# Conditional linear layer with a residual: twelve instead of sixteen slices of the conditioned weights in fp32, their bf16 parts laid out by burst, and loads in another order

## The chip, the core and the metric

One NeuronCore of one Trainium2 chip runs the kernel. The metric is the device time of one execution in microseconds. SyncE and ScalarE issue the transfers, each from a queue of its own; all of them share the core's 16 DMA engines.

## The reference

```python
def reference(x, cond_8, L0_cond_weight, L0_cond_mask, L0_cond_bias):
    # x (128, 128, 512), cond_8 (128, 8), weight (8, 512, 512), mask (512, 512), bias (512,), all fp32
    masked_w = weight * mask[None, :, :]
    w_bot = jnp.einsum('bg,got->bot', cond_8, masked_w)
    return x + jnp.einsum('bnt,bot->bno', x, w_bot) + bias
```

Each of the 128 batches gets its own 512 x 512 matrix, a mix of eight, and multiplies its 128 rows of x with it. The kernel adds the residual by adding the identity to the matrix.

## The kernel before

**Units, steps, groups.** A unit is 32 batches by 128 output columns; there are 16 (`UNITS`), units 0 to 3 for the first 32 batches, and so on. A unit has eight steps, so `n` runs over 128 steps. In step `n`, `group(n)` multiplies four batches of x with their matrices: 16 fp32 matmuls of 128 x 128 x 128, each of which the profile shows as two records of MATMUL. x lies in eight buffers of 1 MB (`xs`), one for four batches, and stays for four units. The first set is x loads 0 to 7, the next is 8 to 15 (`load_x`, at the steps in `X_AT`), and group 32 is the first to use x load 8, group 39 the first to use x load 15.

**Bursts.** The matrices of the next unit are made beside the groups, in bursts: burst `b` makes 16 output columns for 32 batches, eight bursts a unit (`bursts_before(n)` names those that TensorE runs ahead of group `n`). A burst has four chunks of one PSUM bank (`ps1`, six banks). Two kinds exist:
- the first `FB` = 16 bursts, units 0 and 1, in fp32 (`first_burst`, line 529). Eight run before step 0. VectorE evicts them, times the mask (line 465), and GpSimd adds the identity (`add_one`, line 374);
- the other 112 in bf16 (`burst`, line 549), with the masked weights split in three bf16 parts (w1, w2, w3) and the conditioning values too. ScalarE evicts them (line 406). The contraction has 98 rows: 6 products of parts (`Y_PART`) of 16 rows each, and two rows of the identity (`eye`). So a slot of `ring` holds, by partition, w1, w2, w1, w2, w1, w3 and the identity.

**Parts.** A tile is 128 x 512 masked weights; there are 32 of them, in 8 halves of 4, a half for 4 bursts. For tile `t`, SyncE loads it (`load_raw`, two at a time), VectorE multiplies the mask (line 449), ScalarE casts to w1 (line 397), GpSimd subtracts (line 365) and makes w3 (line 367), ScalarE makes w2 (line 401), and SyncE stores all three to `scratch` in memory (`store_parts`, line 269). `TILES_AT` sets the step in which the engines work at a tile. There are five buffers of parts: the cast of tile `t` waits until tile `t - 5` is stored (`stored`, line 218).

**Loads of a burst.** `load_burst` waits for the four tiles of its half to be stored (while they are first needed) and for its slot in the ring of six, then issues the identity rows (line 286), w1 and w2 in one load of 256 KB to partitions 0 to 31 (line 289), w3, 128 KB to 80 to 95 (line 290), and, for the first 24 bursts (`thrice`), w1 again, 128 KB to 64 to 79 (line 293). VectorE copies partitions 0 to 31 to 32 to 63 (line 455) and, for the other 88 bursts, w1 to 64 to 79 in a second copy (line 457).

**What sets the order.** Each engine runs its list in order, written out by the loops over `n`. SyncE's list is the one in which a wait holds up all transfers behind it, except those that ScalarE issues (stores of the result, line 411).

## Time and profile before

| | |
|---|---|
| three runs, us | 640.91, 646.6, 647.01; median 646.6 |
| the profiled execution | 643.54 us, span 641.1 us |
| granted TensorE clock, mean | 0.997 |
| VectorE, ScalarE, GpSimd busy | 411.7, 297.0, 110.2 us |
| bytes moved | 144.44 MB, 225 GB/s over the span |

The page's 40 slices (16 us each) show TensorE busy from the third slice to the end, GpSimd at work until slice 13, and the DMA engines at their fullest up to slice 15:

```profile
PE   6999999999999899999999999999999999999997
POOL 4594586353431000000000000000000000000000
PEclk9999999999999989999999999999999999999999
DMA  8959979999989796455599984555599985652112
```

To read it: a digit is the busy share of a slice in tenths, PEclk the granted clock, DMA the mean busy share of 16 engines. A share of 1.0 in the windows below says that no DMA engine had a gap. "x32" behind a matmul counts records, two to an fp32 matmul.

### The profile page before, as it was taken

The page shows a single profiled execution, that of the slowest core. Times are in us where ns is not written, and L with a number is a line of the kernel's source. Part 1 is how long each engine was busy: PE and PEld are TensorE (multiplying, and loading weights), DVE is VectorE, ACT ScalarE, POOL GpSimd, SP SyncE. Part 2 cuts the span into 40 slices and gives each one's busy share as a digit, 9 for nine tenths or more (in the row PEclk, how much of TensorE's full clock was granted, in tenths as well). Part 3 has the DMA queues.
Part 4 walks back from the last instruction along what each step waited for, and adds up shares of the span by engine and source line. Part 5 has one row for each costly group of instructions (what it writes and reads, how often), then busy time and mean ns, then how long its engine had stood idle before and what let it go on. Part 6 is the DMA issues. An engine that isn't in the chain of part 4 may idle for free.

```text
span 641.1 us, 18487 instructions
## 1 busy us (share of the span) xinstructions
PE 629.0 (98%) x7808; PEld 594.3 (93%) x7808; DVE 411.7 (64%) x425; ACT 297.0 (46%) x513; POOL 110.2 (17%) x95
## 2 busy tenths in 40 slices
PE   6999999999999899999999999999999999999997
PEld 2466779999999899999999999999999999999997
DVE  4986777556655567766776667666676676667421
ACT  0131226666666354445545545455445544554500
POOL 4594586353431000000000000000000000000000
PEclk9999999999999989999999999999999999999999
DMA  8959979999989796455599984555599985652112
GB/s 319 398 176 358 323 219 295 304 330 308 294 278 329 249 292 198 136 162 153 150 271 299 316 236 139 150 155 160 137 238 316 320 248 141 169 150 97 51 67 82
DMA packets 63649, 144.44 MB, mean 225 GB/s; under 512 B 8078, under 2 KB 33776, under 8 KB 53360
## 3 DMA queue, kind: packets, MB, share of 16 engines
q1 hardware_dynamic: 44624, 109.34, 58.0%
q10 hardware_dynamic: 18944, 33.93, 15.6%
q8 instruction: 62, 1.02, 0.7%
q14 instruction: 19, 0.16, 0.1%
HBM read 97.10 MB, written 46.14 MB: 223 GB/s over the span
## 4 chain that ended last, share of the span: by engine, by line
PE 93%; DMA 3%; DVE 2%; issue 1%; ACT 1%; SPq 0%; ACTq 0%; DVEq 0%
PE ps L568 70%; PE ps L549 15%; PE ps L529 7%; DMA w_parts<-parts 2%; DVE wbot L465 1%; DVE raw L449 1%; ACT wbot L406 1%; DMA first_sb<-in_first 1%; DMA ring<-w_parts 1%; DVE ring L457 0%; DVE yblk L484 0%; DVE staged L478 0%; SPq L301 0%; SPq L286 0%; DVE ring L455 0%
## 5 line engine op out<-in xcount | busy, mean ns | idle before, releaser
L568 PE MATMUL ps<-wbot,xs 128*128 128x128 f32 x4096 | 478.2, 277 | 0.8 <-DVE wbot L465 0.4
L568 PEld LDWEIGHTS ps<-wbot,xs 128*128 128x128 f32 x4096 | 466.0, 193 | 5.5 <-issue 4.7
L406 ACT ACTIVATE wbot<-ps 128x512 f32<-128x512 f32 x448 | 259.5, 610 | 224.2 <-PE ps L568 115.8
L478 DVE TENSOR_TENSOR staged<-ps,bias_sb 128x512 f32<-128x512 f32 x128 | 88.5, 691 | 197.8 <-PE ps L568 197.6
L455 DVE COPY ring<-ring 32x4096 bf16<-32x4096 bf16 x112 | 137.2, 1225 | 7.3 <-DMA ring<-w_parts 3.9
L549 PE MATMUL ps<-ydiag,ring 98*128 98x64 bf16 x3584 | 117.2, 193 | 2.8 <-DVE ring L457 2.5
L549 PEld LDWEIGHTS ps<-ydiag,ring 98*128 98x128 bf16 x3584 | 114.8, 98 | 4.3 <-issue 2.6
L457 DVE COPY ring<-ring 16x4096 bf16<-16x4096 bf16 x88 | 107.2, 1218 | 2.7
L365 POOL TENSOR_TENSOR raw<-raw,parts 128x512 f32<-128x512 f32 x32 | 45.7, 1428 | 68.9 <-ACT parts L397 68.8
L465 DVE TENSOR_TENSOR wbot<-ps,ring 128x512 f32<-128x512 f32 x64 | 43.1, 687 | 14.1 <-PE ps L529 10.4
L397 ACT ACTIVATE parts<-raw 128x512 bf16<-128x512 f32 x32 | 19.7, 623 | 50.4 <-DVE raw L449 33.3
L367 POOL TENSOR_TENSOR parts<-raw 128x512 bf16<-128x512 f32 x32 | 39.1, 1221 | 2.5
L449 DVE TENSOR_TENSOR raw<-raw,mask_sb 128x512 f32<-128x512 f32 x32 | 36.6, 1155 | 0.5
L401 ACT ACTIVATE parts<-raw 128x512 bf16<-128x512 bf16 x32 | 20.0, 625 | 35.3 <-POOL raw L365 33.0
L529 PE MATMUL ps<-yblk,xs 128*128 128x512 f32 x64 | 30.2, 636 | 5.2 <-DVE yblk L484 5.2
L529 PEld LDWEIGHTS ps<-yblk,xs 128*128 128x128 f32 x64 | 13.0, 205 | 21.6 <-issue 15.6
L529 PE MATMUL ps<-yblk,ring 128*128 128x512 f32 x64 | 28.6, 592 | 0.0
L529 PEld LDWEIGHTS ps<-yblk,ring 128*128 128x128 f32 x64 | 11.6, 190 | 12.0 <-issue 11.7
L374 POOL TENSOR_TENSOR wbot<-wbot,first_sb 128x512 f32<-128x512 f32 x16 | 20.8, 1300 | 7.4 <-DVE wbot L465 7.2
L484 DVE TENSOR_TENSOR yblk<-first_sb 128x512 f32<-128x512 f32 x1 | 0.7, 691 | 4.5 <-DMA first_sb<-in_first 4.5
L397 ACT ACT_TABLE_LOAD x1 | 1.3, 1283 | 2.7 <-issue 2.7
L355 POOL TENSOR_SCALAR staged<-staged,pick_sb 98x128 bf16<-98x128 bf16 x3 | 1.8, 602 | 0.3
(10 smaller groups left out, 4.0 us busy)
## 6 DMA issues: line engine op xcount, KB each, us to landing
xs<-in_x SPq DMA_DIRECT2D x32, 1024.0 KB, 12.0
out<-staged ACTq DMA_DIRECT2D x128, 256.0 KB, 4.0
ring<-w_parts SPq DMA_DIRECT2D x112, 256.0 KB, 5.7
ring<-w_parts SPq DMA_DIRECT2D x136, 128.0 KB, 6.6
w_parts<-parts SPq DMA_DIRECT2D x32, 384.0 KB, 9.3
raw<-in_w SPq DMA_DIRECT2D x16, 512.0 KB, 9.3
ring<-in_w SPq DMA_DIRECT2D x4, 512.0 KB, 14.9
ring<-in_eye SPq DMA_DIRECT2D x112, 16.0 KB
```

The costliest lines, as they stand in the source:

```text
L365: eng.tensor_tensor(at, at, w1, ALU.subtract).then_inc(s_rest, 1)
L367: eng.tensor_tensor(parts[:, t % PARTN, 2, :, :], at, high_half(t), ALU.subtract).then_inc(s_p3, 1)
L397: eng.activation(parts[:, t % PARTN, 0, :, :], raw[:, t % RAWN, :, :], ACT.Copy).then_inc(s_p1, 1)
L406: eng.activation(chunk_place(b, k), chunk_sums(b, k), ACT.Copy).then_inc(s_ev_a, 1)
L449: eng.tensor_tensor(at, at, mask_sb[:, h % 2, :].unsqueeze(1).to_broadcast([P, TG, TW]), ALU.mult).then_inc(s_mul, 1)
L455: eng.tensor_copy(ring[2 * ROWS:4 * ROWS, i, :], ring[0:2 * ROWS, i, :]).then_inc(s_dup, 1)
L457: eng.tensor_copy(ring[4 * ROWS:5 * ROWS, i, :], ring[0:ROWS, i, :]).then_inc(s_dup, 1)
L465: eng.tensor_tensor(at, ps1[(b * KT + k) % S1B][:, :].rearrange("p (b o) -> p b o", o=CO), mask_t_sb[:, k, o:o + CO].unsqueeze(1).to_broad ...
L478: eng.tensor_tensor(staged[:, n % OUTB, :].rearrange("p (b o) -> p b o", b=GB), ps2[n % S2B][:, :].rearrange("p (b o) -> p b o", b=GB), bi ...
L529: ins = eng.matmul(ps1[(b * KT + k) % S1B][:, :], raw01_sb[u][:, c, k * P:(k + 1) * P], yblk[:, :], start=True, stop=True)
L549: ins = eng.matmul(ps1[at % S1B][:, g * W * OJ:(g + 1) * W * OJ], ring[0:KALL, i, k * CW + g * P:k * CW + (g + 1) * P], ydiag[:, first:fir ...
L568: ins = eng.matmul(ps2[n % S2B][:, b * SL:(b + 1) * SL], xs[:, load % GROUPS * GB + b, k, :], at, start=(k == 0), stop=(k == KT - 1))
```

## The change

Only bursts 0 to 11 are made in fp32 (`FB` = 12, a unit and a half). Bursts 12 to 15, the second half of slice 1, are made from bf16 parts; the order of the halves is turned so that theirs is prepared first. Bursts 12 and 13 stand ahead of group 6, 14 and 15 ahead of group 7, and step 5 has none. `scratch` is laid out by burst: for each of the four bursts of a half its w2, w1 and w3, 16 rows of 8 KB each, one behind the other. So one load takes w2 and w1 (to partitions 0 to 31), another w1 and w3 (to 64 to 95), each 256 KB from memory without a gap, and every burst has both; the three-load form and VectorE's second copy are gone. A tile now holds 512 columns of one kind in place of two times 256, so a store writes runs of 1 KB and not of 512 bytes, and a mask is 256 KB and not 128 (its multiplication reads it without repeating). `TILES_AT` takes tiles 6 to 15 a little earlier and tiles 17 to 31 at closer steps; a tile is stored one step behind its making (two from step 8 on); before, it was two throughout. SyncE issues x loads 2 to 5 ahead of the first stores, x load 6 behind them, x load 7 in step 0, and within a step stores ahead of x loads. The second set's x loads stand at steps 26, 27, 29, 30, 31, 33, 34, 35 in place of 25, 26, 27, 28, 30, 31, 32, 34. `yblk` and the fp32 weights of unit 1 move within the ring.

The core of the diff:

```diff
-FB = FU * CS
+FB = CS + CS // 2
...
 HALVES = 2 * SLICES
+CH = CS // 2
 TG = 2
 TILES = HALVES * NG // TG
 PER_HALF = NG // TG
-TW = 256
-HCOLS = P // OJ * TW
+TW = 512
...
+PART1, PART2, PART3 = 1, 0, 2
...
 EARLY = 4
-TILES_AT = {0: (4, 5), 1: (6,), 2: (7, 8), 3: (9,), 4: (10, 11), 5: (12,), 6: (13, 14), 7: (15,),
-            **{8 + (t - 16) * 7 // 5: (t,) for t in range(16, TILES)}}
+TILES_AT = {0: (4, 5), 1: (6, 7), 2: (8, 9), 3: (10, 11), 4: (12,), 5: (13,), 6: (14,), 7: (15,),
+            **{8 + (t - 16) * 5 // 4: (t,) for t in range(16, TILES)}}
+STORE_AT = {}
+for _n, _tiles in TILES_AT.items():
+    STORE_AT[_n + (1 if _n < GROUPS else 2)] = STORE_AT.get(_n + (1 if _n < GROUPS else 2), ()) + _tiles
...
     if n < GROUPS:
-        return ((), (8,), (9,), (10,), (11,), (12,), (13,), (14, 15))[n]
+        return ((), (8,), (9,), (10,), (11,), (), (12, 13), (14, 15))[n]
...
-X_AT = {_g: LAST_USE[_g - _g % GROUPS - GROUPS] + 1 + _g % GROUPS * 9 // 7 for _g in range(GROUPS, XLOADS)}
+X_AT = {_g: LAST_USE[_g - _g % GROUPS - GROUPS] + 2 + (_g % GROUPS * 4 + 1) // 3 for _g in range(GROUPS, XLOADS)}
...
-    return 2 * ((s - FU) % SLICES) + c // KT
...
+    return (2 * s + c // CH - FB // CH) % HALVES
+def fresh(b):
+    return b < FB + SLICES * CS
...
-    return (half_of(u % SLICES, c) + 1) * PER_HALF if u < FU + SLICES else 0
+    return (half_of(u % SLICES, c) + 1) * PER_HALF if fresh(b) else 0
...
-    return (4, 5, 0, 2, 3, 1)[(b - FB) % RING]
-def thrice(b):
-    return b < FB + 3 * CS
+    return (4, 5, 0, 3, 2, 1)[(b - FB) % RING]
...
 def free_before(b):
     r = b - FB
-    if r < 3:
+    if r < 4:
         return 0
-    if r == RING - 1:
-        return GROUPS
     last = FB - 1 if r < RING else b - RING
-    return next(n for n in range(STEPS) if LAST_BURST[n + 1] >= last)
+    return next(n for n in range(STEPS) if LAST_BURST[n + 1] >= last) + (r == RING - 1)
...
-        yblk = sb("yblk", [P, BANK], fp32)
...
-                    ring[:, 2:4, :].rearrange("p i c -> p (i c)").bitcast(fp32).rearrange("p (c t) -> p c t", c=CS)]
+                    ring[:, 2, :].bitcast(fp32).rearrange("p (c t) -> p c t", c=FB - CS)]
+        yblk = ring[:, 1, BW // 2:BW // 2 + 2 * BANK].bitcast(fp32)
...
-                at = scratch[h, 0, i, 0, :]
-                to = bass.AP(tensor=at.tensor, offset=at.offset, ap=[[TW, P], [ROWS // TG * HCOLS, 3 * TG], [1, TW]])
-                eng.dma_start(to, parts[:, t % PARTN, :, :, :].rearrange("p j g c -> p (j g) c"))\
-                   .then_inc(s_store[t % PARTN], 16)
+                at = scratch[h, 0, 0, i * TG * OJ, :]
+                to = bass.AP(tensor=at.tensor, offset=at.offset, ap=[[TW, P // CH], [3 * ROWS * BW, CH], [ROWS * BW, 3], [1, TW]])
+                eng.dma_start(to, parts[:, t % PARTN, :, :]).then_inc(s_store[t % PARTN], 16)
             def load_burst(b):
                 u, c = divmod(b, CS)
                 s, i = u % SLICES, slot_of(b)
                 h = half_of(s, c)
-                if u < FU + SLICES:
+                if fresh(b):
                     for t in range(h * PER_HALF, (h + 1) * PER_HALF):
                         stored(eng, t)
                 if b >= FB + RING:
                     eng.wait_ge(s_s1, (b - RING + 1) * KT)
-                elif b >= FB + 5:
+                elif b == FB + 5:
                     eng.wait_ge(s_ev_v, FB * KT)
-                elif b >= FB + 3:
+                elif b == FB + 4:
                     eng.wait_ge(s_s1, FB * KT)
                 ones = (KT - 1 - s) * CW // 2
                 eng.dma_start(ring[KROWS:KALL, i, :].bitcast(fp32), eye[c, :, ones:ones + BW // 2]).then_inc(s_eye[i], 16)
-                w1_w2 = scratch[h, 0:2, :, :, c % KT * BW:(c % KT + 1) * BW].rearrange("j g o c -> (j g o) c")
-                w3 = scratch[h, 2, :, :, c % KT * BW:(c % KT + 1) * BW].rearrange("g o c -> (g o) c")
-                eng.dma_start(ring[0:2 * ROWS, i, :], w1_w2).then_inc(s_w12[i], 16)
-                eng.dma_start(ring[5 * ROWS:KROWS, i, :], w3).then_inc(s_w3[i], 16)
-                if thrice(b):
-                    w1 = scratch[h, 0, :, :, c % KT * BW:(c % KT + 1) * BW].rearrange("g o c -> (g o) c")
-                    eng.dma_start(ring[4 * ROWS:5 * ROWS, i, :], w1).then_inc(s_w1[i], 16)
+                w21 = scratch[h, c % CH, 0:2, :, :].rearrange("j r c -> (j r) c")
+                w13 = scratch[h, c % CH, 1:3, :, :].rearrange("j r c -> (j r) c")
+                eng.dma_start(ring[0:2 * ROWS, i, :], w21).then_inc(s_w21[i], 16)
+                eng.dma_start(ring[4 * ROWS:KROWS, i, :], w13).then_inc(s_w13[i], 16)
...
-            load_x(2)
-            load_first(1, 4, 2)
-            load_x(3)
+            for g in range(2, 6):
+                load_x(g)
             for t in range(EARLY):
                 store_parts(t)
+            load_x(6)
             loaded = FB
             kept = 0
             for n in range(STEPS):
-                kept = max((kept, EARLY if n >= 2 else 0, *(t + 1 for t in TILES_AT.get(n - 3, ()))))
-                if n + X_AHEAD < GROUPS:
-                    load_x(n + X_AHEAD)
-                if n == 0:
-                    load_first(1, 6, 2)
+                kept = max((kept, EARLY if n >= 1 else 0, *(t + 1 for t in STORE_AT.get(n - 1, ()))))
                 for t in (8, *TILES_AT[RAW_AHEAD]) if n == 0 else TILES_AT.get(n + RAW_AHEAD, ()):
                     if t >= RAWN and t % 2 == 0:
                         load_raw(t)
+                if n == 0:
+                    load_x(7)
                 while loaded < BURSTS and free_before(loaded) <= n and tiles_of(loaded) <= kept:
                     load_burst(loaded)
                     loaded += 1
+                for t in STORE_AT.get(n, ()):
+                    store_parts(t)
                 for g in range(GROUPS, XLOADS):
                     if X_AT[g] == n:
                         load_x(g)
-                for t in TILES_AT.get(n - 2, ()):
-                    store_parts(t)
...
-                if not thrice(b):
-                    eng.tensor_copy(ring[4 * ROWS:5 * ROWS, i, :], ring[0:ROWS, i, :]).then_inc(s_dup, 1)
...
-                if n == GROUPS - 2:
-                    duplicate(FB)
-                    made += 1
-                while n >= GROUPS and made < BURSTS and made <= n + GROUPS + AHEAD:
+                while n >= GROUPS // 2 and made < BURSTS and made <= n + GROUPS + (AHEAD if n > GROUPS // 2 else 0):
```

SyncE's list from the first stores of tiles on, before (`w_parts` is the scratch in memory; eye, w1 and w2, w3, w1 again are the four loads of a burst; the burst here is 16, then follow 17 and 18 in the same form):

```order
L269 DMA w_parts<-parts 128x6x256 [waits s_p3,s_p2] x4
...
L301 DMA xs<-in_x 128x2048 [waits s_s1]
L246 DMA mask_sb<-in_mask 128x256 [waits s_mul]
L256 DMA raw<-in_w 128x1024 [waits s_p3,s_p2]
L286 DMA ring<-in_eye 2x2048 [waits s_store2,s_store3,s_store1,s_store0]
L289 DMA ring<-w_parts 32x4096
L290 DMA ring<-w_parts 16x4096
L293 DMA ring<-w_parts 16x4096
...
L269 DMA w_parts<-parts 128x6x256 [waits s_p3,s_p2] x2
L301 DMA xs<-in_x 128x2048 [waits s_s1]
```

and now (the burst is 12, then 13, 14 and 15 in the same form; line 266 stores tiles, 294 loads x, 242 a mask, 252 tiles, 282 to 286 a burst):

```order
L266 DMA w_parts<-parts 32x12x512 [waits s_p3,s_p2] x4
...
L294 DMA xs<-in_x 128x2048 [waits s_s1]
L242 DMA mask_sb<-in_mask 128x512 [waits s_mul]
L252 DMA raw<-in_w 128x1024 [waits s_p3,s_p2]
L282 DMA ring<-in_eye 2x2048 [waits s_store2,s_store3,s_store1,s_store0]
L285 DMA ring<-w_parts 32x4096
L286 DMA ring<-w_parts 32x4096
...
L266 DMA w_parts<-parts 32x12x512 [waits s_p3,s_p2] x4
L252 DMA raw<-in_w 128x1024 [waits s_p3,s_p2]
```

Behind the first four stores, four bursts of two loads stand ahead of the next stores (tiles 4 to 7, four in a row), where three bursts of three loads stood ahead of two.

ScalarE's list ahead of its first eviction, before (line 401 makes w2, 397 casts w1 and waits for a stored tile, 411 stores a result, 406 evicts; the steps are 6 to 8):

```order
L401 ACTIVATE parts<-raw 128x512 [waits s_rest]
L397 ACTIVATE parts<-raw 128x512 [waits s_store3,s_mul]
L397 ACTIVATE parts<-raw 128x512 [waits s_store4,s_mul]
L411 DMA out<-staged 128x512 [waits s_o]
L401 ACTIVATE parts<-raw 128x512 [waits s_rest] x2
L397 ACTIVATE parts<-raw 128x512 [waits s_store0,s_mul]
L406 ACTIVATE wbot<-ps_4 128x8x32x2 [waits s_s2,s_s1]
L406 ACTIVATE wbot<-ps_5 128x8x32x2 [waits s_s2,s_s1]
L411 DMA out<-staged 128x512 [waits s_o]
```

and now (line 392 makes w2, 388 casts w1, 402 stores, 397 evicts; the steps are 4 to 6):

```order
L392 ACTIVATE parts<-raw 128x512 [waits s_rest] x2
L388 ACTIVATE parts<-raw 128x512 [waits s_store2,s_mul]
L402 DMA out<-staged 128x512 [waits s_o]
L392 ACTIVATE parts<-raw 128x512 [waits s_rest]
L388 ACTIVATE parts<-raw 128x512 [waits s_store3,s_mul]
L397 ACTIVATE wbot<-ps_0 128x8x32x2 [waits s_s2,s_s1]
L397 ACTIVATE wbot<-ps_1 128x8x32x2 [waits s_s2,s_s1]
L402 DMA out<-staged 128x512 [waits s_o]
```

The first eviction by ScalarE (burst 16 before, burst 12 now) has moved up past the work at tiles 14 and 15: it stands behind the cast of tile 13 and ahead of that of tile 14, where it stood behind the cast of tile 15.

## Rows read from the trace of the kernel before

**Rows 1.** The page, part 1: busy us, share of the span, instructions.
```profile
PE 629.0 (98%) x7808; PEld 594.3 (93%) x7808; DVE 411.7 (64%) x425; ACT 297.0 (46%) x513; POOL 110.2 (17%) x95
```

**Rows 2.** The page, part 5: second copies on VectorE; count, busy, mean ns, idle before.
```profile
L457 DVE COPY ring<-ring 16x4096 bf16<-16x4096 bf16 x88 | 107.2, 1218 | 2.7
```

**Rows 3.** The chain in order of time: start us, us, what was waited for or worked.
```profile
68.46 3.44 PE ps L529 x8
...
82.47 6.87 PE ps L529 x16
...
92.91 0.94 PE ps L549 x32
...
204.31 13.15 DMA w_parts<-parts
...
217.91 3.47 DMA ring<-w_parts
...
225.22 8.86 PE ps L568 x64
...
240.53 3.65 PE ps L568 x32
```

**Rows 4.** Timeline of TensorE: start us, us, work, count, idle before and releaser.
```profile
224.13 1.09 PE L549 MATMUL ps<-ydiag,ring 98*128 98x64 bf16 x32 [2.46 <-DVE ring L457]
```

**Rows 5.** Windows: us; busy of each engine; clock, DMA share, GB/s.
```profile
10.00:30.00 20.00, 20.00 (x47) 8.75 (x47) 16.89 (x25) 1.89 (x3) 12.34 (x14) 1.00 1.02 417
...
60.00:70.00 10.00, 10.00 (x58) 7.15 (x57) 5.99 (x9) 0.00 (x0) 0.00 (x0) 1.00 1.06 257
...
80.00:90.00 10.00, 10.00 (x47) 6.17 (x46) 7.29 (x8) 2.76 (x6) 9.76 (x9) 1.00 0.72 245
...
100.00:200.00 100.00, 99.70 (x1421) 98.95 (x1420) 59.03 (x59) 67.35 (x119) 45.22 (x32) 1.00 1.00 304
...
200.00:220.00 20.00, 20.00 (x251) 19.98 (x250) 12.16 (x12) 9.57 (x17) 0.00 (x0) 1.00 0.85 286
...
260.00:320.00 60.00, 60.00 (x864) 59.89 (x864) 41.42 (x40) 30.64 (x53) 0.00 (x0) 1.00 0.52 148
```

**Rows 6.** Timeline of SyncE: start us, us, DMA issued.
```profile
54.42 0.42 SPq L293 DMA_DIRECT2D ring<-w_parts  x1
...
57.79 0.42 SPq L293 DMA_DIRECT2D ring<-w_parts  x1
...
58.31 0.97 SPq L269 DMA_DIRECT2D w_parts<-parts  x2
...
224.07 0.42 SPq L301 DMA_DIRECT2D xs<-in_x  x1
```

**Rows 7.** Their landings, one line each: L293 twice, L269 (first), L301.
```profile
DMA to landing us min/median/max: 9.9/9.9/9.9
...
DMA to landing us min/median/max: 11.6/11.6/11.6
...
DMA to landing us min/median/max: 12.1/12.1/12.1
...
DMA to landing us min/median/max: 15.5/15.5/15.5
```

**Rows 8.** The page, part 6: x loads, KB each, median us to landing.
```profile
xs<-in_x SPq DMA_DIRECT2D x32, 1024.0 KB, 12.0
```

**Rows 9.** Timeline of ScalarE at the cast of tile 9.
```profile
70.53 0.63 ACT L397 ACTIVATE parts<-raw 128x512 bf16<-128x512 f32 x1 [13.53 <-DMA w_parts<-parts]
```

**Rows 10.** Timeline of GpSimd: the two subtractions of tile 9; one identity added.
```profile
71.24 1.16 POOL L365 TENSOR_TENSOR raw<-raw,parts 128x512 f32<-128x512 f32 x1 [12.67 <-ACT parts L397]
...
72.47 1.04 POOL L367 TENSOR_TENSOR parts<-raw 128x512 bf16<-128x512 f32 x1
...
90.77 1.16 POOL L374 TENSOR_TENSOR wbot<-wbot,first_sb 128x512 f32<-128x512 f32 x1
```

**Rows 11.** Waits of SyncE: us in total, times, longest.
```profile
SPq L218 <- DMA w_parts<-parts: 18.0, 2, 12.4
```

60 lines of the change are left out of this document (26 added, 34 removed).

## The prediction

> **What bounds the kernel now.** I read the page first: TensorE is busy for 629.0 of the span of 641.1 us [rows 1]. So only two things can move the end: less work on TensorE, or other waits of it. The second view is the chain in order of time [rows 3]. It shows what a step costs: an fp32 burst on TensorE 3.44 us (the two of step 7 together 6.87), a bf16 burst 0.94, a group of sixteen fp32 matmuls 3.65. It also shows the one place where TensorE is not the chain: at 204.31 a store of tile 31 is issued, lands 13.15 us later, and only then may the load of burst 44 be issued (3.47 to land); its copy and burst 44 itself follow. TensorE waits 2.46 us for that [rows 4], and the two groups behind it take 8.86 us where two at 3.65 would take 7.3: 1.6 us of lower clock after the wait. So 4.1 us of the span are lost there.
>
> Third, who was late in that place? The windows [rows 5] say: the transfer queues. From 60 to 70 and from 100 to 200 us their share is 1.0 or above; from 260 us on, with no tiles to load or store and no x loads, it is 0.52. Up to 240 us the kernel stands close to two limits, TensorE's and the queues', and after that at TensorE's alone.
>
> **What goes: four fp32 bursts.** Bursts 12 to 15 become bf16: 4 x (3.44 - 0.94) = 10.0 us of TensorE time. With the 4.1 us of waiting gone too, the span would be 641.1 - 4.1 - 10.0 = 627.0. The 88 second copies on VectorE go as well, 107.2 us of it [rows 2]; nobody waited for VectorE but once, at 224, and there for a copy that was itself late by its load. I cost them at nothing; what hides them is TensorE's groups.
>
> **What is added to the queues.** Each bf16 burst now takes two loads of 256 KB, onto 32 partitions each. The nearest rows are the bursts of before that took the same bytes, to the same partitions, in three loads: the last piece of burst 16 is issued at 54.42 and lands 9.9 later, that of burst 18 at 57.79 and 11.6 later [rows 6, 7]. That is 64.3 and 69.4: two bursts in 5.1 us of a full queue, 2.56 each. An x load, 1 MB to 128 partitions, costs 2.5 at the 417 GB/s of the window from 10 to 30 us [rows 5]; in the window from 60 to 70, which is mostly bursts, the same full queue moved 257 GB/s. So bytes of bursts are dear. What the change adds up to x load 15, the last of the second set of eight, needed at group 39:
> - bursts 12 to 15 loaded: 4 x 2.56 = +10.2
> - bursts 40 to 48 load a third piece again, a quarter of 2.56: 9 x 0.64 = +5.8
> - x loads 4 and 5 are ahead of the first store, where the queue has room: -5.0; 512 KB of fp32 weights gone: -1.3
> - six masks of twice the size, 128 KB more each: +1.9
> - 28 stores of the same bytes in half as many pieces. No row shows a store in pieces of 1 KB. Its gain lies between nothing and half of the 0.9 us that 384 KB take at 417 GB/s; I take 0.1 each, since the queue's full windows already move other loads with small pieces among them: -2.8 (ends 0 and -13)
>
> Sum +8.8. Before, x load 15 was issued at 224.07 and landed 15.5 later, at 239.6 [rows 6, 7]; group 39 started at 240.53 [rows 3]. The queues had idle time that a later TensorE would let them use: 2.8 us in 80 to 90 and 3.0 in 200 to 220 [rows 5]. So x load 15 lands at 239.6 + 8.8 - 5.8 = 242.6. Group 39 without waits would start at 240.5 - 4.1 - 10.0 = 226.4. TensorE is thus late by some 16 us there, in several waits, not one: **the gain of 10 us is handed to a queue that cannot go faster.** Behind group 39 the queue has room again: the two later sets of x loads meet no tiles, and 12.0 us of median landing [rows 8] stand against at least four steps of 3.65 to 5.5 us between issue and use.
>
> **The first of these waits, at step 6.** The store of tile 4 is now issued behind four bursts. Before, it was issued at 58.31 and landed 12.1 later, at 70.4 [rows 6, 7], and ScalarE stood 13.53 us for it, in front of its cast of tile 9 [rows 9]. In the changed order the queue ahead of it holds 1.5 MB of x and fp32 weights less (-3.8), a mask's 128 KB more twice (+0.6) and one burst more (+2.6): it lands near 69.8. Behind that cast ScalarE has, before it may evict burst 12: casts of tiles 9 to 13, and these wait for GpSimd, which takes 1.16 + 1.04 for each tile [rows 10] and two additions of the identity of about 1.15 between. From the landing: 0.6 + 2.3 + 1.15 + 2 x 2.3 + 1.15 + 1.2 + 2 x 0.6 = 12.2. Eviction starts at 82.0. TensorE gets to burst 12 at 72.0 (68.46, where the fp32 burst 12 started before, and one group ahead of it) and has six banks, so it stands from 73.4, in the middle of burst 13, until the first eviction ends at 82.6: 9.2 us. Before, VectorE evicted these bursts and no cast stood in front of them. This wait is part of the 16 us and not to be added, since the queue works on meanwhile.
>
> **The sum.** 627.0 + 16.2 + 2 x 1.6 for the clock, lowered after the two longest waits as at 225, = 646.4 of span. The profiled execution took 643.5 at a span of 641.1, so 2.4 lie around it: 648.8. The median of the runs shown is 646.6, so against that the change is +0.3%. About 1% is what a measurement of this kernel can tell from no change: below 640.1 I call faster, above 653.1 slower.
>
> **A rule to weigh.** The row says 2.56 us for 512 KB onto 32 partitions twice, half the rate of x loads. The Trainium skill, "SBUF — State Buffer", section "Door 1: The DMA port swizzle", says that 32 partitions reach 8 of 16 ports, and gives 189 GB/s; by that a burst would cost 2.8 us, an estimate, and the new order in memory would not help. The trace's 2.56 is near it. By the same page 16 partitions reach half as many ports again, so a load of half the bytes would take as long as the full one; the landings of the three pieces do not settle that.
>
> **Rivals.**
> - *Reads from memory were the brake (faster).* Before, a burst's rows lay 32 KB apart; now they lie together. For it: the low rate occurs only with these loads (but so does the narrow destination). Against it: the weights' rows of the fp32 part lie apart too and moved at full rate within the window of 10 to 30 us. If it holds, a burst costs 1.3 us at 417 GB/s, 37 bursts save 46 us, and the queues bind nowhere. The wait at step 6 stays, smaller: the store lands at 69.8 - 4 x 1.26 = 64.8, the first eviction ends at 77.6, 4.2 us late. 627.0 + 4.2 + 1.6 + 2.4 = 635.2.
> - *The third piece is free.* If a load onto 16 partitions already cost what one onto 32 costs, the 5.8 fall away: 643.0. This is the port rule above carried through (same page and section).
> - *SyncE stands for the landing of stores (slower).* Each half's first burst waits until the half's last tile is stored, and SyncE issues nothing meanwhile; at 204 to 218 this let the queue run dry once, 3.5 us from the new load to its landing. In the changed order the store is issued one step ahead of that burst, as before, but the queue is fuller, and x loads 10 to 15 stand behind the last such wait instead of 14 and 15. If three more halves run the queue dry: 3 x 3.5 = 10.5, less the 2 or so that the sum already grants: 657. It decides from the point at which a store lands more than a step after its issue, some 4.6 us; the one at 58.31 took 12.1.
> - *The change doesn't take the fp32 work off the path* is excluded: TensorE's order shows it.
>
> **How the numbers follow.** Forecast (queues full, price of a burst as before) 0.36, its own range 643 to 653; free third piece 0.10; memory reads 0.33; SyncE's standing 0.21. Faster by over 1%: the 0.33 and a little of bursts near 2 us, 0.34. Within 1%: 0.45. Slower: 0.21. Range 634 to 657: from the faster rival to the slower one. The term that decides is the price of a burst: at 1.3 the queue has 30 us to spare, at 2.56 it lacks 16, and it turns near 2.1.
>
> **What will show each step.**
> - TensorE busy about 10 us less for lines of stage 1: 0.94 per burst for 12 to 15.
> - Landings of the two pieces of bursts 12 to 15: 2.5 us from burst to burst means the forecast, 1.3 the faster rival.
> - ScalarE's cast of tile 9 near 70 us (65 in the faster rival), and TensorE's wait inside burst 13 until 82.6 (77.6).
> - Waits of TensorE for x loads at groups 34 to 39, and for the copy of burst 40, with a lowered clock behind them. If TensorE has no wait past 100 us, the queue's account is wrong.
> - After group 39 both profiles should show equal steps: eight groups and eight bursts in 8 x (3.65 + 0.94) = 36.7 us.
> - SyncE's waits for landings of stores: 18.0 us in two waits before [rows 11]; far more would be the slower rival.

## The result, and the profile after

The changed kernel takes 667.6 us (median of 4 runs, 662.8 to 668.4) against 646.2 for the kernel before on the same chip (640.9 to 647.0): a ratio of 1.033, 95% interval 1.026 to 1.041. The prediction was 648.8, or +0.3%, its range 634 to 657; it gave its largest chance (0.45) to a time within 1% of before. The change is 3.3% slower. Here and below, medians are over all executions, and ratios are of the means without the few executions in which the chip was in a slower state.

| | before | after |
|---|---|---|
| span of the profiled execution, us | 641.1 | 660.9 |
| mean granted TensorE clock | 0.997 | 0.985 |
| TensorE busy | 629.0 | 625.5 |
| group 39 starts at | 240.4 | 250.7 |
| from there to the end of the span | 400.7 | 410.3 |

TensorE's busy time fell by the 10.0 us of fp32 work that went, and grew again by the lowered clock (below). The last two lines divide the loss: of the 19.8 us of span, 10.3 are there when group 39 starts, and 9.5 come behind it, where the prediction saw equal steps.

The waits of TensorE in the changed kernel: us in total, times, longest.

```profile
PE ps L551 <- DMA xs<-in_x: 14.1, 6, 4.6
PE ps L532 <- ACT wbot L397: 11.3, 1, 11.3
```

The timeline of TensorE, the rows with an idle time in front of them (start, us, work, count, idle before and releaser), and group 39:

```profile
84.70 1.10 PE L532 MATMUL ps<-ydiag,ring 98*128 98x64 bf16 x16 [11.27 <-ACT wbot L397]
85.61 5.15 PE L551 MATMUL ps<-wbot,xs 128*128 128x128 f32 x32
...
226.87 3.84 PE L551 MATMUL ps<-wbot,xs 128*128 128x128 f32 x32 [0.74 <-DMA xs<-in_x]
234.59 5.46 PE L551 MATMUL ps<-wbot,xs 128*128 128x128 f32 x32 [3.88 <-DMA xs<-in_x]
...
244.41 5.47 PE L551 MATMUL ps<-wbot,xs 128*128 128x128 f32 x32 [2.49 <-DMA xs<-in_x]
...
250.65 3.82 PE L551 MATMUL ps<-wbot,xs 128*128 128x128 f32 x32
...
393.41 3.84 PE L551 MATMUL ps<-wbot,xs 128*128 128x128 f32 x32 [1.32 <-DMA xs<-in_x]
...
535.36 3.84 PE L551 MATMUL ps<-wbot,xs 128*128 128x128 f32 x32 [1.04 <-DMA xs<-in_x]
545.67 5.47 PE L551 MATMUL ps<-wbot,xs 128*128 128x128 f32 x32 [4.61 <-DMA xs<-in_x]
```

One wait of 11.3 us in burst 13, three waits for x loads in the first later set (7.1), three in the two sets behind it (7.0). Where the kernel before had one wait of 2.5 [rows 4], this one has seven. A group takes 5.46 us for 3.82 where behind a wait the granted clock is at half for a part of it (0.50, the level of 1.2 GHz, from 547 to 549 us): the four such groups (5.15, 5.46, 5.47 and 5.47 against some 3.83) cost 6.2.

The windows show who was late (busy of each engine; clock, DMA share, GB/s):

```profile
70.00:80.00 10.00, 3.43 (x67) 3.30 (x65) 7.54 (x6) 2.63 (x5) 9.77 (x7) 0.91 0.69 222
80.00:100.00 20.00, 15.30 (x202) 15.24 (x203) 6.05 (x6) 13.70 (x26) 10.23 (x10) 0.79 1.00 308
...
140.00:180.00 40.00, 39.85 (x582) 39.42 (x580) 25.95 (x25) 27.07 (x49) 20.57 (x15) 1.00 0.91 283
...
220.00:240.00 20.00, 15.38 (x169) 14.95 (x168) 5.72 (x6) 5.44 (x10) 0.00 (x0) 0.91 1.03 310
```

While TensorE stood in burst 13, the transfer queues were not full either: 0.69 of their time from 70 to 80 us. Around 220 to 240 they are full, and TensorE waits for them. The page's issues tell the same (KB each, median us to landing); before it was 12.0 [rows 8]:

```profile
xs<-in_x SPq DMA_DIRECT2D x32, 1024.0 KB, 16.9
```

Behind group 39 it is the same. The stretch of the next set of x loads, 16 to 23, before the change and then after it:

```profile
340.00:380.00 40.00, 40.00 (x552) 39.93 (x551) 28.10 (x28) 19.12 (x33) 0.00 (x0) 1.00 0.99 286
380.00:400.00 20.00, 20.00 (x320) 19.96 (x316) 14.21 (x14) 10.91 (x19) 0.00 (x0) 1.00 0.51 143
```

```profile
340.00:380.00 40.00, 40.00 (x546) 39.94 (x545) 17.18 (x18) 19.72 (x34) 0.00 (x0) 1.00 1.02 303
380.00:400.00 20.00, 18.57 (x282) 18.29 (x281) 7.63 (x8) 9.46 (x17) 0.00 (x0) 1.00 1.02 312
```

Before, the queues have worked the set off by 380 us or so (0.51 from there on); now they are full for all 60 us, and TensorE waits at 393.41.

From issue to landing, the eight x loads issued between 181 and 219 us in the changed kernel took:

```profile
DMA to landing us min/median/max: 9.3/19.8/30.6
```

### The profile page after: what moved, and what is told of

It reads as the page before. It is cut to its first block, busy times and chain, and to the rows that moved or that the text cites. A ratio compares the mean times of both kernels' runs of the same rounds, so it can differ in the third digit from the quotient of the medians.

```text
span 660.9 us, 18561 instructions
## 1 busy us (share of the span) xinstructions
PE 625.5 (95%) x7904; PEld 597.5 (90%) x7904; DVE 303.4 (46%) x325; ACT 303.9 (46%) x529; POOL 107.3 (16%) x91
## 3 DMA queue, kind: packets, MB, share of 16 engines
q10 hardware_dynamic: 18944, 33.93, 15.7%
## 4 chain that ended last, share of the span: by engine, by line
PE 77%; DMA 14%; DVE 3%; POOL 2%; SPq 1%; issue 1%; ACT 1%; ACTq 0%; DVEq 0%
PE ps L551 60%; PE ps L532 13%; DMA xs<-in_x 11%; PE ps L514 3%; DMA w_parts<-parts 2%; DVE raw L440 1%; DVE wbot L453 1%; ACT wbot L397 1%; POOL raw L356 1%; POOL parts L358 1%; DMA first_sb<-in_first 1%; SPq L286 1%; POOL wbot L365 0%; SPq L285 0%; DVE ring L445 0%
## 5 line engine op out<-in xcount | busy, mean ns | idle before, releaser
L551 PE MATMUL ps<-wbot,xs 128*128 128x128 f32 x4096 | 483.6, 279 | 15.0 <-DMA xs<-in_x 14.1
L397 ACT ACTIVATE wbot<-ps 128x512 f32<-128x512 f32 x464 | 267.0, 609 | 247.7 <-PE ps L551 130.5
L445 DVE COPY ring<-ring 32x4096 bf16<-32x4096 bf16 x116 | 142.4, 1228 | 3.6
L532 PE MATMUL ps<-ydiag,ring 98*128 98x64 bf16 x3712 | 121.7, 194 | 11.6 <-ACT wbot L397 11.3
L388 ACT ACTIVATE parts<-raw 128x512 bf16<-128x512 f32 x32 | 19.8, 625 | 41.9 <-DVE raw L440 26.6
L453 DVE TENSOR_TENSOR wbot<-ps,ring 128x512 f32<-128x512 f32 x48 | 32.3, 687 | 8.8 <-PE ps L514 8.7
L514 PE MATMUL ps<-ring,xs 128*128 128x512 f32 x64 | 29.9, 631 | 5.5 <-DVE ring L472 5.5
L514 PEld LDWEIGHTS ps<-ring,xs 128*128 128x128 f32 x64 | 12.9, 203 | 21.7 <-issue 15.5
L365 POOL TENSOR_TENSOR wbot<-wbot,first_sb 128x512 f32<-128x512 f32 x12 | 16.0, 1339 | 6.3 <-DVE wbot L453 6.2
L514 PE MATMUL ps<-ring 128*128 128x512 f32 x32 | 14.4, 593 | 0.0
L514 PEld LDWEIGHTS ps<-ring 128*128 128x128 f32 x32 | 5.8, 191 | 5.7 <-issue 5.7
## 6 DMA issues: line engine op xcount, KB each, us to landing
raw<-in_w SPq DMA_DIRECT2D x16, 512.0 KB, 10.0
```

The lines of the kernel that those rows point to most:

```text
L388: eng.activation(parts[:, t % PARTN, PART1, :], raw[:, t % RAWN, :], ACT.Copy).then_inc(s_p1, 1)
L397: eng.activation(chunk_place(b, k), chunk_sums(b, k), ACT.Copy).then_inc(s_ev_a, 1)
L445: eng.tensor_copy(ring[2 * ROWS:4 * ROWS, i, :], ring[0:2 * ROWS, i, :]).then_inc(s_dup, 1)
L453: eng.tensor_tensor(at, ps1[(b * KT + k) % S1B][:, :].rearrange("p (b o) -> p b o", o=CO), mask_t_sb[:, k, o:o + CO].unsqueeze(1).to_broad ...
L514: ins = eng.matmul(ps1[(b * KT + k) % S1B][:, :], raw01_sb[u][:, c, k * P:(k + 1) * P], yblk, start=True, stop=True)
L532: ins = eng.matmul(ps1[at % S1B][:, g * W * OJ:(g + 1) * W * OJ], ring[0:KALL, i, k * CW + g * P:k * CW + (g + 1) * P], ydiag[:, first:fir ...
```

## The experiments

Seventeen kernels were run. Ratios are against runs of the kernel before on the same chip, whose median was between 643.5 and 645.0 (646.2 for the changed kernel). "Tail" is the profiled span less the start of group 39. It comes from one execution each, and single executions of one kernel differ by up to some 10 us here, so a tail or a wait locates a loss and the ratio sizes it.

| kernel | median us | ratio, 95% interval | group 39 | tail |
|---|---|---|---|---|
| changed | 667.6 | 1.033 [1.026, 1.041] | 250.7 | 410.3 |
| e1 before, third piece for all bursts | 650.2 | 1.009 [1.006, 1.013] | 244.6 | 403.7 |
| e2 before, late x loads | 640.5 | 0.997 [0.994, 1.001] | 242.0 | 400.8 |
| e10 before, both | 660.8 | 1.025 [1.018, 1.031] | 244.6 | 409.8 |
| e9 changed, early x loads | 654.7 | 1.017 [1.011, 1.024] | 251.1 | 407.3 |
| e4 changed, stores first | 660.6 | 1.028 [1.021, 1.036] | 246.7 | 410.3 |
| e8 changed, VectorE evicts | 666.1 | 1.037 [1.031, 1.043] | 249.4 | 415.2 |
| e11 changed, early x, stores first | 647.9 | 1.007 [1.003, 1.010] | 243.6 | 402.2 |
| e12 changed, a quarter of later x | 641.8 | 0.997 [0.995, 1.000] | 238.8 | 400.8 |
| e5 changed, copy from burst 40 | 658.3 | 1.025 [1.017, 1.032] | 255.9 | 400.8 |
| e14 early x, stores first, VectorE, pieces | 643.6 | 0.998 [0.994, 1.001] | 237.4 | 401.0 |

**Is it the queue at all?** Taken first here though it ran later, since it carries the rest. In `load_x`:

```diff
-                eng.dma_start(xs[:, at:at + GB, :, :], x[g]).then_inc(s_x[g % GROUPS], 16)
+                count = GB if g < GROUPS else 1
+                eng.dma_start(xs[:, at:at + count, :, :], x[g, :, 0:count, :, :]).then_inc(s_x[g % GROUPS], 16)
```

> The changed kernel, but each of the 24 x loads of the later sets brings only 256 KB of its 1 MB (three quarters of the later x stay those of the first set, so the output is not the reference's). It takes 18 MB off the queue and nothing from any engine. Queue theory: all six waits for x loads (14.1 us) and their lowered groups (about 5) go, and the wait in burst 13 (11.3) with its lowered groups stays: span 627.0 + 11.3 + 3 = 641, 643 to 645 with what lies around it. If something else lies under the x waits (ScalarE, GpSimd, SyncE's standing), it appears in their place and the time stays above 650.

Measured: span 639.6, time 641.8, ratio 0.997. The waits of TensorE, but for the one at the start of the program and three below half a microsecond, are down to one:

```profile
PE ps L533 <- ACT wbot L398: 10.7, 1, 10.7
```

All six waits for x are gone, and nothing took their place. So the 14.1 us and their lowered clock are a matter of the bytes in the queue, and the wait in burst 13 is another matter. SyncE's waits for stores came to 31.0 us in this kernel (22.7 in the changed one) and cost TensorE nothing.

**Bytes or the time of issue?** A square of four: the third piece for all bursts or not, and the later x loads early or late, first in the kernel before.

```diff
-    return b < FB + 3 * CS
+    return b < BURSTS
```

> The kernel before, with part 1 loaded a second time for all bursts (84 more loads of 128 KB, and VectorE's 88 second copies gone). Theory A, the burst's bytes fill the queues in the later x sets: in the changed kernel a burst lands every 2.2 us, so eight of them take 17.6, eight x loads of 1 MB 20.0 and eight stores of the output at 0.75 another 6, in a unit of 36.7 us; the third piece is a quarter of the burst. Then TensorE waits for x loads in the second and third set here too, 4 to 7 us in all, and with two groups at the lower clock the time is 651 to 656. Theory B, the x loads are only issued too late: these are issued as in the kernel before, so nothing changes, 645 to 648. In both, the wait at burst 44 (2.46 us) may grow by up to 1 us.

```diff
-X_AT = {_g: LAST_USE[_g - _g % GROUPS - GROUPS] + 1 + _g % GROUPS * 9 // 7 for _g in range(GROUPS, XLOADS)}
+X_AT = {_g: LAST_USE[_g - _g % GROUPS - GROUPS] + 2 + (_g % GROUPS * 4 + 1) // 3 for _g in range(GROUPS, XLOADS)}
```

> The kernel before, with nothing changed but the steps at which the 24 later x loads are issued: those of the changed kernel (steps 26, 27, 29, 30, 31, 33, 34, 35 for the first set instead of 25 to 34, one step later for most). Theory B: TensorE waits for them, as in the changed kernel, 14.1 us in six waits there; 655 to 662. Theory A: a load takes 12.0 us in the median here and has three or four steps of 4.6 us, so it is in time but for the last one or two of the first set; 646 to 650.

> The other corner: the kernel before with both, the third piece for all bursts and the late x loads. If the two work together, the later sets wait 5 to 9 us here as in the changed kernel, and behind group 39 it takes 407 to 412: 653 to 658. If they only add up (1.1 and 0), 402, and 648 to 651.

Measured: +0.9% for the bytes, -0.3% (an interval that holds none) for the late x loads, +2.5% for both. Neither theory of the first two runs was right by itself. The tails say where: 403.7 with the bytes (1.6 of it is group 39's own lowered clock, 1.1 a wait in the last set), 400.8 with late x, 409.8 with both. The timeline of TensorE in the kernel with both has the later sets' waits of the changed kernel:

```profile
232.74 5.60 PE L568 MATMUL ps<-wbot,xs 128*128 128x128 f32 x32 [6.04 <-DMA xs<-in_x]
...
381.67 3.84 PE L568 MATMUL ps<-wbot,xs 128*128 128x128 f32 x32 [1.03 <-DMA xs<-in_x]
391.15 6.56 PE L568 MATMUL ps<-wbot,xs 128*128 128x128 f32 x32 [3.78 <-DMA xs<-in_x]
...
540.62 3.84 PE L568 MATMUL ps<-wbot,xs 128*128 128x128 f32 x32 [0.69 <-DMA xs<-in_x]
```

The queues' own account gives the price of a third piece. Part 3 of the page (packets, MB, share of 16 engines) in the kernel with the third piece for all bursts:

```profile
q1 hardware_dynamic: 47440, 120.88, 66.8%
q10 hardware_dynamic: 18944, 33.93, 16.6%
```

83.4% of 648.3 us is 540.7; before it was 58.0 and 15.6%, or 471.9 us of 641.1. The edit adds 88 pieces of 128 KB (bursts 40 to 127; 11.54 MB by the page, not the 84 of the expectation), and the queues' time grew by 68.8 us, 0.78 for each. The prediction had 0.64. The 0.78 is not the piece's own time alone: 7.6 of the 68.8 us are on ScalarE's queue (q10, 15.6% of 641.1 and 16.6% of 648.3), which moves the same packets and bytes in both, so other transfers' packets took longer too.

The same square from the other side, the changed kernel with the x loads back at the early steps (the diff above, turned round):

> The changed kernel, with nothing but the steps of the 24 later x loads set back to those of before. So far the bytes alone (all bursts with the third piece, x loads early) made the later sets wait 1.1 us, the late x loads alone 0, and the changed kernel has both and waits 7.0. If they work together, behind group 39 this kernel needs 401 to 404 instead of 410.3, and x load 15 is in the queue ahead of one or two bursts more, so group 39 starts 1 to 3 us earlier than 250.7: 656 to 660. If the bytes of the changed kernel alone fill the later sets, 410 stays and the time is 665 to 668.

Measured: 654.7, ratio 1.017: half of the loss is gone by this one line. The tail fell from 410.3 to 407.3 only, and group 39 didn't come earlier (251.1), in a profile that fell on the slowest of the kernel's four executions (660.2). That part of the expectation failed, and where all of the gain lies isn't shown by this profile. A wait of 2.8 us for burst 40's load is new at 208.8, since SyncE now stands longer for stores that lie behind x loads in the queue (us in total, times, longest):

```profile
SPq L214 <- DMA w_parts<-parts: 38.5, 5, 11.2
```

**The wait in burst 13: a loss of its own, or handed to the queue?** First the stores of tiles 4 and 5 go ahead of bursts 12 to 15:

```diff
+                if n == 1:
+                    for t in STORE_AT[1]:
+                        store_parts(t)
                 while loaded < BURSTS and free_before(loaded) <= n and tiles_of(loaded) <= kept:
...
-                for t in STORE_AT.get(n, ()):
+                for t in STORE_AT.get(n, ()) if n != 1 else ():
```

> The changed kernel, with the stores of tiles 4 and 5 issued ahead of the loads of bursts 12 to 15 in step 1, not behind them. The store of tile 4 then lands four bursts of 2.2 us earlier, at 60 instead of 68.6, ScalarE's chain in front of the eviction of burst 12 ends near 75 instead of 84, and TensorE's wait of 11.3 us there falls to 2 to 4. If the step-6 wait is a loss of its own: 8 us and one lowered group less, 657 to 659. If the queue is the limit up to x load 15, as the prediction had it: x load 15 lands at 249 as before, the waits for x loads grow by what the first one loses, and the time stays within 2 us of 667.5.

Measured: 660.6. The wait fell from 11.3 to 6.0, group 39 started at 246.7 for 250.7, and the waits for x stayed (14.3). Between the two theories, nearer to the second: of 5.3 us and their clock 4 reached group 39. What moved it is the window of the stall:

```profile
70.00:80.00 10.00, 4.03 (x79) 3.85 (x79) 6.09 (x5) 4.78 (x10) 9.21 (x7) 0.87 1.07 362
```

The queues are full there now (1.07 for 0.69). TensorE is idle for as long as before in this window, but the stores and tile loads that hang on ScalarE's casts are not held up.

The other way to take the wait away leaves the stores where they are:

```diff
-    return b < FB
+    return b < 2 * CS
...
+                    if b >= FB:
+                        eng.tensor_copy(chunk_place(b, k), chunk_sums(b, k)).then_inc(s_ev_v, 1)
+                        return
```

> The changed kernel, but VectorE evicts bursts 12 to 15 as it did before the change (now by a copy, since they come masked). No cast stands in front of them, so TensorE's wait of 11.3 us in burst 13 goes, and some 1.6 of lower clock. If the queue sets the time of group 39 (x load 15 landed at 249.3 and the group started at 250.7), the waits for x loads grow by about as much: 664 to 667, x load 15 at 247 to 249. The run with the stores first gave back 5.3 of that wait and x load 15 came only 2.7 earlier. If the wait is a loss of its own: 654 to 656.

Measured: 666.1, as the queue's theory had it. The 11.3 us became four waits of at most 2.4 around bursts 12 to 15, 5.1 in all, and the waits for x grew from 14.1 to 18.9 us. TensorE's own lateness at step 6 is worth nothing while a queue is behind it; the lateness of the stores is worth something.

Both mended edits together:

> The changed kernel with x loads as early as before and the stores of tiles 4 and 5 ahead of bursts 12 to 15. The stores first took 5.3 off TensorE's wait in burst 13 and 3.9 off the span. If the two gains are independent, this is 3 to 4 us under the run with early x loads alone, 652 to 656. If early x loads only shift the backlog onto the store of tile 31, for which SyncE stands (46 us in five waits in the combined kernel, and then 10.3 us at burst 40), the gain is smaller and such a wait of 2 us or more appears near 213.

Measured: 647.9, ratio 1.007, 19.7 us under the changed kernel. By medians the gains add up, 12.9 and 7.0 us; by ratios they are 1.6 and 0.5%, and 2.7% here, which is about their sum within intervals of 0.7%. The tail is 402.2, two waits for x are left of six (1.5 and 4.1).

**Fewer bytes.** VectorE copies part 1 again for the later bursts. The first attempt kept two loads per early burst, the second of them of part 1 and part 3, which don't lie together in the order that the copy needs:

```diff
-PART1, PART2, PART3 = 1, 0, 2
+PART1, PART2, PART3 = 0, 1, 2
...
-                w13 = scratch[h, c % CH, 1:3, :, :].rearrange("j r c -> (j r) c")
+                w3 = scratch[h, c % CH, 2, :, :]
+                w13 = scratch[h, c % CH, 0:3:2, :, :]
```

> The changed kernel, with part 1 loaded a second time only for the 28 bursts 12 to 39, and copied by VectorE from burst 40 on, as the kernel before did from 36 on. Theory A: the queue loses 128 KB for each of 88 bursts, so the waits for x loads in the second and third set (7.0 us, and some 3 of lower clock) are gone, and those of the first set (7.1) shrink by nine bursts times 0.55 = 5; 650 to 657. Theory B: the x loads are as late as before, so the time stays at 665 to 668.

Measured: 763.8, ratio 1.186, far outside both. From burst to burst the load of 256 KB in front of it landed 6.1 us later (12.0 us from issue at 48.49, 25.5 from issue at 53.23, over three bursts). The same bytes with each load over neighbouring rows:

```diff
-                    eng.dma_start(ring[4 * ROWS:KROWS, i, :], w13).then_inc(s_w13[i], 16)
-                else:
-                    eng.dma_start(ring[5 * ROWS:KROWS, i, :], w3).then_inc(s_w13[i], 16)
+                    eng.dma_start(ring[4 * ROWS:5 * ROWS, i, :], w1).then_inc(s_w1[i], 16)
+                eng.dma_start(ring[5 * ROWS:KROWS, i, :], w3).then_inc(s_w13[i], 16)
```

> As the kernel before last, part 1 loaded twice only for bursts 12 to 39 and copied by VectorE from burst 40 on, but every load is now of whole neighbouring rows in memory: 256 KB and 128 KB, and 128 KB again for the early ones. If the 6.1 us per burst of that run came from its load of two blocks of rows with a third between them, they are gone. Theory A (bytes of bursts): behind group 39 the time to the end, 410.3 us in the changed kernel, falls to the 400.6 of before; x load 15 lands 3 to 5 us earlier than 249.3; 650 to 656. Theory B (x loads issued too late): 665 to 668. If a load onto 16 partitions costs what one onto 32 does, the early bursts are dearer by 0.5 us each than in the changed kernel and x load 15 comes no earlier, 656 to 660.

Measured: 658.3. The tail is 400.8 as before the change: the later sets' loss is gone, with the x loads as late as in the changed kernel. That settles the tail from the third side. Group 39 starts later, at 255.9, with a new wait of 5.1 us for burst 40's copy, so the time lies in the band of the last case and the tail is that of theory A. The two kernels' packets, the strided one first:

```profile
DMA packets 50698, 146.62 MB, mean 192 GB/s; under 512 B 7406, under 2 KB 19792, under 8 KB 40144
```

```profile
DMA packets 51538, 146.62 MB, mean 223 GB/s; under 512 B 8246, under 2 KB 20632, under 8 KB 40984
```

The second has 840 packets more, 30 for each of 28 bursts, and all of them are under 512 B: the packets that carry the data are as many in both. The Trainium skill, "DMA: Bandwidth & Descriptors", section "Why a DMA increments its semaphore by 16 and not by 1", says that a transfer runs on the largest number of engines, at most 16, that divides the slowest dimension of both its patterns, here 2 (two blocks in memory, 32 partitions), and that each engine that takes part posts its own write to the semaphore. The small packets agree with that, if they are these writes: 2 for the load of two blocks, 32 for two loads over 16 engines each. So does the DMA share of the strided kernel: 0.13 from 71 to 73 us, that of two engines of 16, at 49 GB/s. 256 KB at 49 GB/s take 5.3 us of the 6.1.

Then three edits together, and the copy for all bursts:

> The changed kernel with three parts undone: VectorE evicts bursts 12 to 15, part 1 is copied by VectorE from burst 40 on, and the x loads are issued at the steps of before. What is left of the change is the four bursts in bf16, the masks, the layout in memory and the order of the first steps. Queue theory: behind group 39 400.6 us as before; ahead of it x load 15 decides, at 241 to 244; 641 to 646. If the waits are independent losses, all are gone and it is 630 to 633.

Measured: 651.2, ratio 1.014 [1.007, 1.020], 5 us above the queue theory's band. Waits for x: none. In their place stands the slower rival of the prediction: SyncE waits 46.1 us for stores, and burst 40 is loaded, copied and used late:

```profile
192.19 2.56 SPq L308 DMA_DIRECT2D xs<-in_x  x1
206.35 0.25 SPq L293 DMA_DIRECT2D ring<-in_eye  x1
```

```profile
215.08 1.87 PE L553 MATMUL ps<-ydiag,ring 98*128 98x64 bf16 x32 [10.28 <-DVE ring L461]
```

(SyncE's timeline, nothing issued from 194.8 to 206.4; and TensorE's.) The store of tile 31, issued at 190.6 behind 3 MB of x, landed 15.7 later.

> The one before, and part 1 is never loaded a second time: 28 bursts more at 384 KB for 512, all ahead of x load 15. At 0.55 us each that is 15 us of queue. Queue theory: x load 15 is in time, the waits vanish, 629 to 634. If a load onto 16 partitions is no cheaper than onto 32, or if the x loads are not held by the bursts, it equals the one before within 3 us. VectorE has 28 copies of 1.2 us more, between 57 and 240 us, where it is busy about half the time; if its copies come late for a burst, this shows as a wait for them.

Measured: 663.8, ratio 1.034 [1.028, 1.041], 12.6 us slower than the one before, where 629 to 634 or no difference over 3 us was expected. Neither theory. The bytes went (107.8 MB on SyncE's queue), and TensorE waited for ScalarE seven times, 10.5 us, and for VectorE's evictions and copies 12.5 us more (5.3 in the kernel without these copies, besides its 10.3 at burst 40). GpSimd's part of a tile had become slower, with the same instructions (part 5; the kernel before this one first):

```profile
L370 POOL TENSOR_TENSOR raw<-raw,parts 128x512 f32<-128x512 f32 x32 | 45.9, 1435 | 62.2 <-ACT parts L402 61.8
```

```profile
L370 POOL TENSOR_TENSOR raw<-raw,parts 128x512 f32<-128x512 f32 x32 | 51.3, 1602 | 68.4 <-ACT parts L402 68.1
...
L372 POOL TENSOR_TENSOR parts<-raw 128x512 bf16<-128x512 f32 x32 | 51.1, 1597 | 2.5
...
L461 DVE COPY ring<-ring 16x4096 bf16<-16x4096 bf16 x116 | 158.1, 1363 | 3.6
```

The second subtraction took 1258 ns in the one and 1597 in the other, and VectorE's copy, 1218 in the one (and in the kernel before [rows 2]), takes 1363 in the mean with 28 copies more. Both engines' instructions lengthen in the kernel in which they work beside each other more often. SyncE's waits for GpSimd's part of a tile grew from 27.4 to 52.2 us.

**Can it beat the kernel before?** Five more runs, on the base of early x and stores first.

> The changed kernel with early x loads, the stores of tiles 4 and 5 first, and bursts 12 to 15 evicted by VectorE. Of the 6.0 us still lost in burst 13, VectorE's evictions leave 2 to 5 in small waits (4.9 when they stood alone). The tiles' casts no longer wait behind evictions on ScalarE, but the stores are issued no earlier than their casts allow. If group 39's start (243.6 in the run without this) hangs on when the stores of the first ten tiles go out, it stays within 1 us and the time is 646 to 649. If TensorE's own lateness counts, 641 to 645.

Measured: 648.8, ratio 1.008 [1.005, 1.011]; without VectorE's evictions it was 1.007. Its waits for x came to 7.7, and group 39 started at 244.8, 1.2 us later than without them where the first case allowed 1.

```diff
+                    w2, w1, w3 = (scratch[h, c % CH, j, :, :] for j in range(3))
+                    eng.dma_start(ring[0:ROWS, i, :], w1).then_inc(s_w21[i], 16)
+                    eng.dma_start(ring[ROWS:2 * ROWS, i, :], w2).then_inc(s_w2[i], 16)
+                    eng.dma_start(ring[5 * ROWS:KROWS, i, :], w3).then_inc(s_w13[i], 16)
```

> The one before, with bursts from 40 on loaded as three pieces of 128 KB (parts 1, 2, 3 once each) and the second part 1 copied by VectorE; early bursts stay two pieces of 256 KB. Between bursts 40 and x load 15 nine bursts become a quarter smaller. If what counts is bytes, x load 15 lands 3 to 5 us earlier and the wait of 4.1 us at group 39 goes: 639 to 643. If a load onto 16 partitions costs what one onto 32 does, three pieces are half as dear again as two, and TensorE waits at 39 and in the later sets: 650 to 660.

> The run with early x loads and stores first (ScalarE evicts bursts 12 to 15), with the same three pieces of 128 KB from burst 40 on. Against that run, by bytes: 3 to 5 us less, 643 to 645; by partitions: 5 or more slower. The pair with the run before shows whether VectorE's evictions are worth anything once the queue has room: 3 us and a lowered group, or nothing.

Measured: 643.6, ratio 0.998 [0.994, 1.001] for the first, and 648.4, ratio 1.007 [1.003, 1.010], for the second. The first is 1.0% faster than its partner without pieces (1.008): x load 15 landed at 237.3 for 244.8, as bytes say, and TensorE has 0.6 us of waits for x in all. The second was no faster than its partner (1.007 both), though its profiled execution, its fastest, had a span of 641.9 for 645.8 and x load 15 landed at 241.1 for 243.5. Why one pair gains and the other doesn't isn't shown.

What three loads of 128 KB cost against two of 256 KB can be read from the queues' share. For the second pair it is 63.8 and 17.3% of 641.9, or 520.6 us, with pieces, and 63.3 and 16.1% of 645.8, or 512.8 us, without. For the first pair it is 62.8 and 17.4% of 638.4, or 512.0 us, with pieces, and 63.9 and 16.3% of 647.0, or 518.9 us, without. Over 88 bursts that is between 0.09 us more and 0.08 less a burst: a quarter fewer bytes took the same time within 0.1 us a burst.

> The best of the runs so far (early x, stores first, VectorE evicts, three pieces from burst 40), with burst 12 at step 5 and burst 13 at step 6 instead of both at step 6, as the fp32 bursts of the kernel before stood. VectorE evicts a burst in 2.4 us and TensorE makes one in 0.94, so the two behind each other cost waits: 0.96 + 0.19 and 1.82 + 0.19 at the two pairs, 2.3 for a copy behind the second. One pair is taken apart: 1 to 2 us less of span, 0.997 to 0.993 of the time of before. If burst 12's load (landed 61 in the changed kernel) or its copy comes too late for step 5 at 65, a wait takes the place and nothing is won.

> The one before, with the three pieces and VectorE's second copy from burst 32 on. If bytes count, eight bursts more are a quarter smaller, the store of tile 31 lands earlier, and the wait of 2.55 us for burst 40's copy and the 0.6 at group 39 go: 2 to 4 us less, 0.990 of before. If VectorE's copies disturb the tiles' work on GpSimd, as in the run with copies for all bursts (ScalarE's casts late, seven waits of 1.8 us), waits of 1 to 2 us appear between 170 and 200 and it is no faster.

Measured: 644.9, ratio 1.000 [0.997, 1.004], and 645.5, ratio 1.003 [1.000, 1.007]. No gain from either. In the first, waits for copies around bursts 12 to 15 took the place of the ones removed (5.0 us in three), as its second case had it; the second has the wait of 1.8 for ScalarE at 177.9 that the copies for all bursts brought. So the changed kernel can be brought back to the time of the one before, within what was measured, and none of these beat it. All of the runs on the changed kernel keep its masks of twice the size, the new layout of the stores and its steps for the tiles; what these cost or give by themselves isn't shown.

## Why the prediction was wrong

**"After group 39 both profiles should show equal steps": failed, the largest miss in kind.** "Behind group 39 the queue has room again" compared a landing of 12.0 us with four steps, but took the 12.0 from a kernel with early x loads and 384 KB per burst. Both changed at once. In its place the time behind group 39 was 410.3 us for 400.7, with full queues from 340 to 400 us. By rows of the experiments the queue of a unit holds more than its 36.7 us where x loads are issued in it: six x loads at 2.5, eight bursts at 2.2, eight stores of output at 0.75 are an estimate of 38.6 (2.5 from [rows 5], 2.2 from the landings below, 0.75 as 256 KB at 350 GB/s, between the 304 and the 417 of full windows [rows 5]). The prediction made this sum only up to group 39. It also never priced the line `X_AT`, which the diff shows: one step later for most loads. In the kernel before, the bytes alone cost 0.9%, the late issue alone nothing, and both 2.5%, with a tail of 409.8.

**"The queues had idle time that a later TensorE would let them use" (-5.8), and "the queue works on meanwhile": failed.** The windows of 10 us from 50 us to the start of group 39, with the DMA share times the width summed as work and the rest as idle time (the share reads up to 1.08 where it is full, so idle time is somewhat low in every row):

| kernel | work, us | idle, us | group 39 |
|---|---|---|---|
| before | 186.1 | 4.3 | 240.4 |
| changed | 191.3 | 9.3 | 250.7 |
| e4 changed, stores first | 191.0 | 5.7 | 246.7 |
| e9 changed, early x loads | 192.0 | 9.1 | 251.1 |
| e11 changed, early x, stores first | 191.0 | 2.6 | 243.6 |
| e14 early x, stores first, VectorE, pieces | 184.6 | 2.7 | 237.4 |

The prediction's +8.8 of work was +5.2, so less than forecast. Its -5.8 of idle time was +5.0. (With shares over 1 counted as 1, idle time is 9.5 us before and 12.4 after, so +2.9, and +7.3 of work.) Either way none of the idle time was used, and some came to it. Group 39 started at 250.7, not 242.6. In the stall of step 6 alone the queues idled 3 us (0.69 of 10). What feeds the queues is SyncE's list, where the idle time must come from, and SyncE stood 55.4 us for ScalarE's and GpSimd's parts of tiles in the changed kernel (21.4 and 34.0), 35.4 before (9.1 and 26.3). The stores-first runs leave the work as it is and take only idle time away; the pieces take work away.

**The price of a burst: between the forecast and the rival, near the turning point.** Landings of the last pieces of bursts 12 to 15 in the changed kernel (issued from 48.38 to 52.19; the first landed 12.7 us after its issue and the last 15.5):

```profile
L286 SPq DMA_DIRECT2D ring<-w_parts x4: 417/421/504, 48.4 to 52.2; - x4
...
DMA to landing us min/median/max: 12.7/14.1/15.5
```

(52.19 + 15.5 - 48.38 - 12.7) / 3 = 2.2 us a burst, between the forecast's 2.56 and the faster rival's 1.3, near the 2.1 at which the account was said to turn. By the prediction's own account 37 bursts at 2.2 are 13.3 us less of queue, which leaves x load 15 only 3 us late; it landed at 249.3. The idle time above is a part of that. For the rest, the work grew by 5.2 us where the account with 2.2 has -4.5: either the 2.2, the spacing of these four bursts, isn't what a burst costs on the average, or stores and masks were dearer than priced. Which isn't shown. Rows that lie together in memory did not make it an x load's rate, so reads of rows that lie apart were not the whole brake; they may be the difference from 2.56 to 2.2. The Trainium skill's rule, "SBUF — State Buffer", section "Door 1: The DMA port swizzle", that fewer partitions reach fewer ports, had given 2.8 for a burst, an estimate; the measured 2.2 is faster than that, but what the prediction made of it, that a load of half the bytes onto 16 partitions takes as long as the full one onto 32, has the runs half on its side: three loads of 128 KB took the engines' time of two of 256 KB within 0.1 us, so one costs some two thirds of the other, between the half of the bytes and the whole of the rule.

**The second rival (third piece free): wrong.** The queues' time grew by 0.78 us for each, and the kernel's by 0.9% for 88 of them.

**Step 6: mechanism and place right, size short.** Forecast 9.2 us from 73.4 to 82.6, measured 11.3 to 84.7. The store of tile 4 landed at 68.6 (forecast 69.8); the term that was too small is GpSimd. From its first subtraction for tile 9 to the end of that for tile 12 it took 13.6 us (69.34 to 82.97), where the sum has 10.4. Its two subtractions, 1.16 and 1.04 in [rows 10], took nearly twice that while VectorE copied:

```profile
69.34 2.11 POOL L356 TENSOR_TENSOR raw<-raw,parts 128x512 f32<-128x512 f32 x1 [12.97 <-ACT parts L388]
71.53 1.90 POOL L358 TENSOR_TENSOR parts<-raw 128x512 bf16<-128x512 f32 x1
```

```profile
69.22 3.31 DVE L445 COPY ring<-ring 32x4096 bf16<-32x4096 bf16 x2
```

Before, VectorE evicted at that time, and its first copy stood at 79.7. "Part of the 16 and not to be added" was half right: taking the wait away at VectorE gave nothing, halving it at the stores gave 7 us by medians, 0.5% by ratios.

**SyncE standing for stores (the slower rival, 0.21): not the cause here, and real.** 22.7 us in five waits for 18.0 in two [rows 11], and with the x loads shrunk 31.0 us of it cost nothing. It came out when 3 MB of x stood in the queue ahead of tile 31's store: 10.3 us at burst 40 in the combined kernel. What made half of the loss, later sets short of queue, was not on the list of rivals.

**The clock: one item short.** Two lowered groups were forecast before group 39, three came, and one behind it; the mean fell from 0.997 to 0.985. The sum should not have had its 3.2 us at all: by its own account x load 15 sets the start of group 39, and lowered groups ahead of it only shorten a wait. Without them the forecast span is 643.2, and the measured 660.9 is 17.7 more: 8.1 at group 39 and 9.6 behind it.

**Four fp32 bursts gone, 10.0 us: right.** The fp32 bursts' matmuls took 44.3 us for 58.8, those of the bf16 bursts 121.7 for 117.2, which is 10.0 us less. With transfers taken away the span was 639.6 with a wait of 10.7 in it and its lowered clock, within 2 us of 627.0 plus these.

## What to carry to other kernels

Make the queue's sum for every stretch that repeats, not only for the one that is full now, and make it with the kernel's new issue times: here the bytes alone cost 0.9%, the later issue alone nothing, and both 2.5%. A stall on one engine does not let the queue catch up unless what feeds the queue (casts, stores, the issuing engine's waits) runs on; ask which wait holds the stores, and sum work and idle time of the queue by windows before counting on the idle time. An engine that gets work "at nothing" beside another should be checked for the other's durations in the rows.

## What was not expected of the hardware

- A load of 256 KB in two blocks of 16 rows, with a gap between, moved 49 GB/s at a DMA share of 0.13, that of two engines of 16, and a burst took 6.1 us for 2.2.
- GpSimd's subtraction over 128x512 took 1.16 us in [rows 10] and 2.1 beside VectorE's copies; with 28 more copies, all beside tiles, the mean of the second subtraction rose from 1258 to 1597 ns.
- Three loads of 128 KB onto 16 partitions each took the engines' time of two of 256 KB onto 32 within 0.1 us a burst.
- SyncE's issue of a transfer, mostly 0.3 to 0.6 us, took 5.0 us for an x load at 59.34 in the kernel before and 8.3 us for a store near 54.8 in the changed one, both where the DMA share was above 1, and up to 3.0 us for one of x loads 8 to 15 where they are early (e9).
